# A gated cross-attention block on one core: the head re-ordered, small preparations moved between engines, fillers on TensorE

## What is computed

```python
x = x + tanh(g_xattn) * attention(layernorm(x), ctx, ctx, mask, W1, b1, W2, b2)
#   q = (layernorm(x) @ W1.T + b1) @ W2.T + b2 ; k = (ctx @ W1.T + b1) @ W2.T + b2
#   softmax(q @ k.T / sqrt(128) + mask) @ ctx
x = x + tanh(g_ffn) * ffn(layernorm(x))
#   quant(a) = clip(round(a * 16)) / 16 in 8 bits, weights and biases with 64
#   h = relu(quant(quant(x) @ quant(w1).T + quant(b1)))          hidden size 512
#   out = quant(h) @ quant(w2).T + quant(b2)
```

## Time and profile before

| | |
|---|---|
| median of 3 runs | 72.86 us (72.84 to 75.65) |
| profiled execution | 72.85 us, of which its instructions span 71.1 us |
| busy: TensorE, VectorE, ScalarE, GpSimd | 58.8, 57.9, 48.7, 45.0 us |
| granted clock of TensorE | 1.00 of full |
| moved by DMA | 8.96 MB |

### The profile page before, as it was taken

How to read it: one execution, slowest core, us unless ns; L and a number is a source line. 1 busy time by engine, 2 the same in 40 slices (tenths; PEclk the granted TensorE clock), 3 DMA queues, 4 the chain that set the end, 5 groups by cost and what they waited for, 6 DMA issues and landing times.

```text
span 71.1 us, 1754 instructions
## 1 busy us (share of the span) xinstructions
PE 58.8 (83%) x493; PEld 45.3 (64%) x497; DVE 57.9 (81%) x319; ACT 48.7 (69%) x133; POOL 45.0 (63%) x90
## 2 busy tenths in 40 slices
PE   4951944986899899997999999999999999798920
PEld 4851622633488579796495898787978869286410
DVE  4888930374989999999999999999999999984630
ACT  0000075188356969899999999997988969769800
POOL 5101599029695699999897999499995918540000
PEclk9999999999999999999999999999999999999999
DMA  0979999999999980000000200300403003033123
GB/s 2 243 163 318 311 380 276 298 256 285 296 237 262 274 192 21 0 5 0 5 5 9 74 0 0 148 0 0 148 9 148 0 24 128 0 146 125 69 75 111
DMA packets 5546, 8.96 MB, mean 126 GB/s; under 512 B 744, under 2 KB 3153, under 8 KB 5537
## 3 DMA queue, kind: packets, MB, share of 16 engines
q1 hardware_dynamic: 5247, 8.66, 41.9%
q10 hardware_dynamic: 290, 0.19, 1.0%
HBM read 6.75 MB, written 2.10 MB: 125 GB/s over the span
## 4 chain that ended last, share of the span: by engine, by line
PE 27%; POOL 23%; DVE 23%; ACT 11%; issue 10%; ACTq 1%; POOLq 0%; DVEq 0%
POOL xq L334 12%; PE bank_T L379 8%; POOL rs L316 7%; ACT pr L509 4%; DVE st L557 4%; DVE h L548 4%; PE bank_T L391 3%; PE bank_O L455 3%; POOL xn L324 3%; PE bank_S L399 3%; PE bank_A L415 3%; DVE x_sb L646 3%; PE bank_H L440 2%; DVE sc L634 2%; ACT kpT L494 2%
## 5 line engine op out<-in xcount | busy, mean ns | idle before, releaser
L535 ACT ACTIVATE h<-bank_H,fb_q 128x512 int8<-128x512 f32 (+2 forms) x27 | 15.5, 643 | 1.5 <-PE bank_H L440 1.1
L324 POOL TENSOR_SCALAR xn<-x_sb,nm,rs 128x128 f32<-128x128 f32 x32 | 14.4, 466 | 0.8
L557 DVE BATCH_NORM_STATS2 st<-x_sb 128x6 f32<-128x128 f32 x64 | 14.0, 277 | 0.0
L509 ACT ACTIVATE pr<-sc,mn 128x120 f32<-128x120 f32 x32 | 12.2, 388 | 2.1 <-DVE mn L634 2.1
L334 POOL TENSOR_SCALAR xq<-x_sb,nm,rs 128x128 int8<-128x128 f32 x29 | 12.7, 456 | 1.0 <-POOL rs L316 0.2
L312 POOL TENSOR_TENSOR rs<-ve,half 128x4 f32<-128x4 f32 (+3 forms) x8 | 8.1, 1014 | 5.8 <-DVE nm L564 5.8
L316 POOL TENSOR_TENSOR rs<-ve,half 128x4 f32<-128x4 f32 (+2 forms) x9 | 8.5, 945 | 4.6 <-DVE nm L564 4.6
L379 PE MATMUL bank_T<-kT_sb,Mk 128*128 128x480 f32 (+2 forms) x18 | 9.7, 627 | 1.0 <-ACT xaT L501 0.8
L634 DVE CUSTOM_DVE_ANT_0 sc<-bank_S,mask_neg 128x120 f32<-128x120 f32 x32 | 7.1, 276 | 4.1 <-PE bank_S L399 4.1
L399 PE MATMUL bank_S<-kpT,xaT 128*128 128x120 f32 x64 | 9.4, 289 | 1.0 <-ACT xaT L501 1.0
L399 PEld LDWEIGHTS bank_S<-kpT,xaT 128*128 128x128 f32 x64 | 8.4, 199 | 2.5 <-ACT xaT L501 1.9
(11 more groups left out here) (75 smaller groups left out, 94.4 us busy)
## 6 DMA issues: line engine op xcount, KB each, us to landing
x_sb<-in_x SPq DMA_DIRECT2D x6, 256.0 KB, 8.0
out_y<-y_sb SPq DMA_DIRECT2D x6, 256.0 KB, 2.2
kT_sb<-in_ctx_kT SPq DMA_DIRECT2D x6, 240.0 KB, 8.4
v_sb<-in_ctx_v SPq DMA_DIRECT2D x6, 240.0 KB, 9.3
mp_sb<-in_mlp_par SPq DMA_DIRECT2D x1, 514.0 KB, 6.8
x_sb<-in_x SPq DMA_DIRECT2D x2, 192.0 KB, 12.3
out_y<-y_sb SPq DMA_DIRECT2D x2, 192.0 KB, 1.9
kT_sb<-in_ctx_kT SPq DMA_DIRECT2D x2, 180.0 KB, 12.5
```

Of the source, the lines that this page charges most:

```text
L324: nc.gpsimd.tensor_scalar(xn[g % RING][:, tile(j)], x_sb[:, of(g, j)], nm1[:, of(g, j, 1)], rs1[:, of(g, j, 1)], ALU.add, ALU.mult).then_i ...
L509: nc.scalar.activation(pr[i][:, j, :], sc[i][:, j, :], ACT.Exp, scale=-1.0, bias=mn[:, of(g, j, 1)], accum_out=den[:, of(g, j, 1)]).then_i ...
L535: nc.scalar.activation(low_byte(h16[g % RING], hcols(c, g)), bank_H[c][:, cols(g)], ACT.Relu, bias=fb1_q[:, c:c + 1]).then_inc(h_act[c], 1)
L557: nc.vector.bn_stats(st[:, START[g] + j, :], x_sb[:, of(g, j)]).then_inc(st_done, 1)
```

## The change

Once-only work moves. VectorE keeps one of three memsets of `h16`, GpSimd takes the other two; the four memsets of `pick_h` go, since a plain matrix of ones (`ones_h`, GpSimd) does with constants that are zero except in every 32nd column. The table of ScalarE's functions is loaded at its start by a one-element Exp. The load of the mask is issued ahead of that of the gate row, and the mask is negated on ScalarE. The fold has one matmul for matrix and bias together, and one VectorE instruction less. The gates are spread ahead of the fold. The first group's keys get a bank of their own (`bank_H[0]`), so its transposes don't wait for `kp_out` and group 1's keys can be projected at once. Of the network's weights ScalarE widens `w1_q` and GpSimd the rest; the bias row is copied out by ScalarE and split on GpSimd. `TILES` and the share tables change a little, `rstd1` is made for each group apart, and `DUE` has new numbers. Of zero matmuls there are 46 at the start and 90 more, in nine pieces (`FILLERS`) at places that `DUE` gives; all of them write to `bank_H[3]`.

```diff
-TILES = [2, 4, 4, 4, 4, 4, 4, 3, 3]
-SPANS = [0, 1, 2, 3, 4, 5, 6, 8, 9]
+TILES = [2, 4, 4, 4, 4, 4, 4, 4, 2]
+SPANS = [0, 1, 2, 3, 4, 5, 6, 7, 8, 9]
-XN_ON_POOL = [2, 4, 4, 4, 4, 4, 4, 3, 3]
-XQ_ON_POOL = [2, 4, 4, 4, 4, 4, 4, 2, 1]
-RELU_ON_ACT = [3, 3, 4, 3, 2, 3, 3, 3, 3]
+XN_ON_POOL = [2, 3, 4, 4, 4, 4, 3, 2, 2]
+XQ_ON_POOL = [2, 3, 4, 4, 4, 4, 4, 4, 1]
+RELU_ON_ACT = [3, 4, 3, 3, 2, 3, 3, 3, 3]
+FILLERS = [8, 36, 7, 9, 6, 4, 3, 14, 3]
...
+        def bank_of_keys(g):
+            return bank_H[0] if g == 0 else bank_T
...
-            pool.wait_ge(mask_in, 16)
-            nc.gpsimd.tensor_scalar(mask_neg[:, :], mask_sb[:, :], -1.0, 0.0, ALU.mult, ALU.add).then_inc(mask_up, 1)
+            for i in range(1, RING):
+                nc.gpsimd.memset(h16[i][:, :].bitcast(F32), BYTE_PAIR).then_inc(bytes_pool, 1)
...
+            def widen_weights():
+                pool.wait_ge(quant8, 2)
+                nc.gpsimd.tensor_copy(w2_q[:, :], mp_8[:, C * P:C * (P + D)]).then_inc(quantd, 1)
+                nc.gpsimd.tensor_scalar(fb1_q[:, :], mp_8[:, C * (P + D):], ACT_SCALE / W_SCALE, 0.0, ALU.mult,
+                                        ALU.add).then_inc(quantd, 1)
+                nc.gpsimd.tensor_copy(fb2_q[:, :], fb2_8[:, :]).then_inc(quantd, 1)
+
+            def split_base():
+                pool.wait_ge(corr_cp, 1)
+                nc.gpsimd.tensor_copy(corr_h[:, :], corr[:, :]).then_inc(base_cp, 1)
+                pool.wait_ge(base_cp, 1)
+                nc.gpsimd.tensor_tensor(corr_r1[:, :], corr[:, :], corr_h[:, :], ALU.subtract).then_inc(base_cp, 1)
...
-            keep_warm(44)
+            keep_warm(46)
             def fold_mm1():
                 pe.wait_ge(ap_in, 16)
-                nc.tensor.matmul(bank_H[0][:, 0:D], W2T_sb, W1_sb, start=True, stop=True).then_inc(fold_mm, 1)
-                nc.tensor.matmul(bank_H[1][:, 0:1], W2T_sb, b1_sb, start=True, stop=True).then_inc(fold_mm, 1)
+                nc.tensor.matmul(bank_H[1][:, 0:D + 1], W2T_sb, W1b1_sb, start=True, stop=True).then_inc(fold_mm, 1)
...
             def transpose_x(g):
                 if g == 0:
                     pe.wait_ge(ident_up, 1)
-                pe.wait_ge(kp_out, g + 1)
+                else:
+                    pe.wait_ge(kp_out, g + 1)
...
             act.dma_start(ap_sb[:, :], attn_par).then_inc(ap_in, 16)
+            act.dma_start(mask_sb[:, :], mask).then_inc(mask_in, 16)
             act.dma_start(row_sb[:, :], rows).then_inc(row_in, 16)
-            act.dma_start(mask_sb[:, :], mask).then_inc(mask_in, 16)
+            act.wait_ge(consts, 1)
+            nc.scalar.activation(warm[:, :], half[:, 0:1], ACT.Exp)
...
-            for i in range(RING):
-                nc.vector.memset(h16[i][:, :].bitcast(F32), BYTE_PAIR).then_inc(bytes_up, 1)
-            nc.vector.memset(pick_h[:, :], 0.0).then_inc(pick_up, 1)
-            dve.wait_ge(pick_up, 1)
-            for p in range(3):
-                nc.vector.memset(pick_h[32 * p:32 * p + 1, :], 1.0).then_inc(pick_up, 1)
+            nc.vector.memset(h16[0][:, :].bitcast(F32), BYTE_PAIR).then_inc(bytes_up, 1)
```

More of the change, by code:

```diff
@@ L2 @@
 from contextlib import ExitStack
+from functools import partial
 import concourse.bass as bass
@@ new lines @@
+    spread_gates=[390],
+    fold_mm1=[405],
+    stats1=[436, 611, 834, 1342, 1641, 2127, 2352, 2592, 2808],
+    fold_cp1=[523],
+    rstd1=[536, 756, 998, 1496, 1879, 2273, 2567, 2930, 3531],
+    normalise_pool=[624, 868, 1109, 1618, 2097, 2394, 2800, 3181, 3630],
+    fold_mm2=[630],
+    transpose_x=[680, 1005, 1421, 1877, 2298, 2644, 2999, 3401, 3925],
+    fold_cp2=[743],
+    copy_xT=[756, 1089, 1550, 1942, 2363, 2719, 3064, 3488, 3987],
+    gate=[782],
+    project_keys=[783, 826, 1242, 1620, 2119, 2465, 2789, 3147, 3559],
@@ new lines @@
+    negate_mask=[820],
+    copy_keys=[845, 928, 1344, 1722, 2221, 2567, 2923, 3324, 3692],
+    scores=[909, 1159, 1794, 2019, 2551, 2875, 3233, 3604, 4036],
+    row_maxima=[971, 1261, 1914, 2271, 2727, 3096, 3483, 3726, 4731],
+    exponentials=[1010, 1399, 1990, 2413, 2769, 3135, 3539, 4203, 4900],
+    normalise_dve=[0, 1011, 0, 0, 0, 0, 2898, 3296],
+    transpose_probs=[1068, 1551, 2202, 2690, 3316, 3692, 4079, 4471, 5032],
+    reciprocals=[1100, 1632, 2259, 2952, 3177, 3672, 4224, 4720, 5361],
@@ new lines @@
+    scale_weights=[1137],
+    widen_weights=[1282],
+    copy_probsT=[1294, 1616, 2275, 2979, 3381, 3757, 4144, 4590, 5158],
+    attend=[1352, 1703, 2377, 3059, 3461, 3836, 4237, 4718, 5295],
+    residual=[1480, 1810, 2489, 3191, 3569, 3945, 4345, 4847, 5442],
+    stats2=[1545, 1995, 2961, 3348, 3808, 4092, 4521, 5162, 5578],
+    copy_ident=[1597],
+    rstd2=[1791, 2679, 3716, 4001, 4112, 4407, 4884, 5308, 5679],
+    quantise_pool=[2001, 3042, 3828, 4234, 4528, 4711, 5006, 5429, 5777],
+    transpose_xq=[2105, 3362, 4008, 4446, 4806, 5064, 5340, 5619, 5911],
@@ new lines @@
+    copy_xqT=[2141, 3438, 4071, 4540, 4850, 5107, 5426, 5718, 6010],
+    hidden=[2251, 3735, 4323, 4627, 4941, 5204, 5496, 5788, 6075],
+    fold_base=[2346],
+    relu1=[2622, 3928, 4424, 4789, 5044, 5307, 5599, 5891, 6145],
+    copy_base=[2657],
+    relu0=[2681, 3814, 4367, 4670, 4984, 5247, 5539, 5831, 6107],
+    quantise_dve=[0, 2926, 0, 0, 0, 0, 0, 0, 5766],
+    split_base=[3268],
+    relu2=[3286, 4014, 4481, 4730, 0, 5366, 5658, 5950, 6184],
+    relu_dve3=[3688, 0, 4455, 4774, 5097, 5372, 5668, 5898, 6163],
@@ L79 @@
+    relu3=[0, 3871],
+    mlp_out=[3949, 4123, 4515, 4829, 5086, 5381, 5641, 5922, 6180],
+    result=[4053, 4256, 4655, 4962, 5297, 5514, 5804, 6096, 6286],
+    relu_dve2=[0, 0, 0, 0, 5029],
+    keep_warm0=[389.5],
+    keep_warm1=[629.5],
+    keep_warm2=[782.5],
+    keep_warm3=[1004.5],
+    keep_warm4=[1158.5],
+    keep_warm5=[1351.5],
+    keep_warm6=[1420.5],
+    keep_warm7=[1550.5],
+    keep_warm8=[1619.5],
 )
+FILLERS = [8, 36, 7, 9, 6, 4, 3, 14, 3]
 class Share(list):
@@ L147, in flamingo_gated_block @@
         sixteen_h = sb("sixteen_h", [1, 3 * 32], BF16)
-        pick_h = sb("pick_h", [3 * 32, P], BF16)
+        ones_h = sb("ones_h", [3 * 32, P], BF16)
         Wc = sb("Wc", [D, D])
@@ L449, in mlp_out @@
                 for j in range(TILES[g]):
-                    nc.tensor.matmul(bank_O[:, tile(j)], pick_h[:, :], corr_h[:, :], start=(j == 0), stop=False)
+                    nc.tensor.matmul(bank_O[:, tile(j)], ones_h[:, :], corr_h[:, :], start=(j == 0), stop=False)
                 for c in range(C):
@@ L458, in mlp_out @@
                 mm.then_inc(o_ready, 1)
-            schedule(once=dict(fold_mm1=fold_mm1, fold_mm2=fold_mm2, spread_gates=spread_gates, fold_base=fold_base),
+            schedule(once=dict(fold_mm1=fold_mm1, fold_mm2=fold_mm2, spread_gates=spread_gates, fold_base=fold_base,
+                               **{f"keep_warm{i}": partial(keep_warm, n) for i, n in enumerate(FILLERS)}),
                      transpose_x=transpose_x, project_keys=project_keys, scores=scores,
@@ L537, in relu @@
                 return stage
-            schedule(once=dict(scale_weights=scale_weights, copy_ident=copy_ident, gate=gate),
+            schedule(once=dict(scale_weights=scale_weights, copy_ident=copy_ident, gate=gate, negate_mask=negate_mask,
+                               copy_base=copy_base),
                      copy_xT=copy_xT, copy_keys=copy_keys, exponentials=exponentials, copy_probsT=copy_probsT,
```

173 lines of the change are left out of this document (64 added, 109 removed).

## The result

The changed kernel took 68.27, 68.29, 69.74 and 71.32 us in its four runs, a median of 69.02 against 72.85; the ratio of its two faster runs to the faster ones of the kernel before is 0.9372, 95% interval 0.9355 to 0.939, and all ratios below are formed so. The first profile is of the run of 69.74 us, so I use a second profile too, of the same kernel run again (label a_again, 68.40 us); what they differ in explains the step between 68.3 and 69.7 us.

The account below looks back on a forecast made before the run. VectorE and TensorE were taken as nearly full from 16.96 to 60.00 us, with gaps in the head. Between TensorE's account of -2.0 and VectorE's of -4.1 it took -3.3 from 72.85: 69.5 us, range 68.0 to 70.9.

Parts of the forecast that it names:

- The start: Head up to x's first transposes on TensorE: taken at 9.0 against 8.03 for the first keys before, +1.0 us.
- the late case's clock: Fold's 36 fillers at the lower clock: 2.1 us at 58 ns, half at the higher; x's transposes at 9.5 or 8.4.
- the lower bound: Earliest start of the gates' matmul: 4.07 us, when the 54 fillers that stand first are done.
- The late bound: Gate row's landing behind the mask's load, if it takes the mask's 5.0 us: about 6.6; 5.0 was taken.
- rival 2: Head: row there at 4.1, clock rises within the 36 fillers, full relief: 67.2 us; chance 0.13.
- Rival 1: Head: gate row lands at 6.6 and clock stays low until the first scores: 72.8, 73.6 at worst; chance 0.12.
- TensorE's work: TensorE from x's transposes on: 53.2 us busy, 3.9 idle, last seven filler pieces 2.0; end 66.1, -2.0 us.
- the estimate of 0.7 us: Last 46 fillers on TensorE: by the skill's 62 ns rule they stay at 2.7 us and more, against the change.
- VectorE's work: VectorE: first maxima at 12.9, then 48.2 us of work and 3.6 of waits; end 64.7, -4.1 us.
- A sign that I had named: Middle of the kernel: the prediction is wrong if VectorE starts to wait there; no VectorE gap before 60 us expected.
- the -3.3: Whole kernel: change taken somewhat past the middle between TensorE's account, -2.0, and VectorE's, -4.1 us.
- Rival 4: GpSimd becomes the bound: waits stay at 11.7, new instructions cost twice; last quantised tile at 68.0; 75 us; chance 0.07.

Follow-up runs that it names:

- a_rowfirst: Changed kernel with the gate row's load issued ahead of the mask's, as in the kernel before: 68.17 to 68.94 us, ratio 0.9422 to the kernel before.
- a_nofill: Changed kernel with all nine pieces of fillers out, the 46 at the start kept: 69.82 to 70.43 us, ratio 0.9633 to the kernel before.
- b_fill: Kernel before with 36 fillers ahead of the fold's second half and 24 ahead of the first transposes: 72.83 us, others 73.67 to 75.59, ratio 1.0197.
- a_foldfill: Changed kernel without the last seven pieces of fillers (46 between real matmuls): 67.87, 68.00, 68.39 and 69.04 us, ratio 0.9344 to the kernel before.
- a_dvework: Changed kernel with the weights' widening and the bias row's split (eight instructions) back on VectorE: 70.01, 71.19, 71.26 and 71.87 us.
- b_table: Kernel before with only the one-element Exp added at ScalarE's start: 71.54, 71.64, 74.15 and 74.31 us, ratio 0.9826.
- v_best: Changed kernel with 18 fillers in the fold, no last seven pieces, gates' matmul and group 2's statistics moved later: 71.65 to 73.11 us, ratio 0.9891 to kernel before.

## Why the prediction was right, and where its sum was off

**The start** was forecast at 9.0 with the late case's clock in part; the first profile has x's transposes at 8.39. The gate row landed at about 4.2, not 5.0, nearly at the lower bound. The late bound of 6.6 took the mask's 5.0 us for whatever stands behind another load. But the mask itself, now second in its queue, landed 2.8 us after its issue in the first profile, and 5.2 when it was third again (a_rowfirst). The Trainium skill, DMA: Bandwidth & Descriptors, section on queues, rings and completion order, says that each DMA engine consumes descriptors in ring order; the prediction made the late bound of that, and no run here shows it as a delay of that size (in a_rowfirst, with the row ahead of the mask, the matmul starts only 0.27 us earlier). 36 fillers cost 2.13 against 2.1. The early case (rival 2) is real as well: with the clock up at 4.2 the transposes start at 6.63. Rival 1, both late, was not seen.

**TensorE's work.** The higher clock came before the keys, as taken, but that the fillers brought it isn't shown (a_nofill, b_fill). The last seven pieces cost some 0.1 us of the end (a_foldfill), not 2.0. From the transposes at 8.39 to the end of its last matmul at 65.3 TensorE is busy 54.1 us and idle 2.8, where I had 53.2 and 3.9. At the higher clock 14 of them fill 0.56 us of the timeline of the first profile, 40 ns each. The 62 ns of the Trainium skill, TensorE: Matmul & The Clock Gate, section on the 56 ns, hold with decoding in microcode; at 40 ns each, the estimate of 0.7 us made from them has nothing for it in this trace.

```profile
17.03 0.63 PE L389 MATMUL bank_H<-zeros_h 128*64 128x64 bf16 x14
17.59 0.65 PE L454 MATMUL bank_A<-ident,pr 128*120 128x128 f32 x4
```

**VectorE's work.** First maxima forecast at 12.9, measured 11.61. From there I had 51.8 us to the end of the last result; it is 54.2. This is the step that was mis-sized, by 2.4 us, and its mis-sized term is the waiting. From 11.61 to 65.83 VectorE is busy 47.9 us, near the 48.2 of my sum, but it waits 6.3 us where I had 3.6. I had only taken off the wait for ScalarE's weights and put nothing in for the waits of the new order, of which the 1.64 us for group 1's scores is the longest. A sign that I had named for a wrong prediction, VectorE waiting before 60 us, was there. The miss at the start (1.3 early) and this one (2.4 late) partly cancelled, which is luck. So is a part of the -3.3, which I took between the two accounts without a reason that gives this point. The measured -3.1 lies there, but the chain of the first profile runs 46% over GpSimd, and neither account had that engine in it. That VectorE holds the piece is shown only as far as a_dvework goes: 2.1 us more work on it, taken from GpSimd, made the piece 1.95 longer.

**GpSimd** was priced at 3.4 us more work and 8 us of waits. It has 2.8 more over the span, the 128x512 widening 0.61 us instead of 1.9, and waits that hardly shrank: 4.8 and 4.5 for statistics and 1.5 for ScalarE's weights. Rival 4 named those waits, but at a doubled price of the new instructions, which cost less than taken: its last quantised tile is done at 61.0, not later than 62.99.

```profile
POOL rs L339 <- DVE nm L620: 4.8, 4, 3.3
POOL rs L335 <- DVE nm L620: 4.5, 4, 1.9
POOL w_q L362 <- ACT fb L540: 1.5, 1, 1.5
```

**Loads** were said not to bind. When the clock rises early, they do: VectorE waits 1.25 us for group 2's x at 8.84, and the first maxima are queued behind it.

**The time.** Forecast 69.5; 69.74 in the run of the first profile, whose clock rose late, 68.3 where it rose early. The parts found one at a time: the freed table load 1.4 (b_table, on the kernel before), the own bank 0.9, VectorE's relief 1.95 less 1.2 for the order's waits, an early rise of the clock 0 or 1.4. They sum to 3.1 or 4.5, near the 3.1 and 4.5 us of the two kinds of run. That closeness proves little. The 1.95 less 1.2 is the difference of the pieces, 0.8, by the way it was worked out; the load and the bank make 2.3 of a head that is 2.0 shorter in the first profile, and 0.3 of the gain lies in the tail and is in none of the parts.

## What to carry to other kernels

Subtract two milestones in both profiles before anything else. If the stretch between them keeps its length, as here over heads from 9.87 to 12.50 us, a change of the head is worth what it does to the first milestone. When work is taken off a busy engine, its waits have to be priced too: the work came out within 0.3 us here, the waits were 2.7 off. In these kernels the table load went where the first activation's waits put it, 1.4 us of the end; see in the timeline what the load waits for. What small fillers bring isn't settled here: 60 of them did nothing for the kernel before. Before a step is moved behind another, look who is queued behind it on the same engine.

## What the runs showed of the hardware that I had not expected

The clock's rise is not at one place for one program: 4.2 and about 9 us in two executions of the same kernel, 1.4 us in the time. Nor did work without a gap bring it: in b_fill TensorE was busy for 7.84 of the 8.08 us from 3.72 to 11.80, and the clock rose only at about 16. The windows of the head give 1.00 although a matmul of 480 columns took 1014 ns there, the lower level, and some 570 to 600 at the higher; they show 0.50 only where the clock had risen before and fallen (b_table, 8 to 12 us). It can fall again: in b_table and v_best slices show 5 after a rise at some 4 us. A filler of 64 columns took 58 ns of the queue at the lower level and 35 to 40 at the higher. A memset of 128x1024 costs GpSimd 0.96 us, about VectorE's 0.91, and widening 128x512 from int8 0.61 us against 0.42 on VectorE.
